# A 48-byte scratch tile declared earlier, so that sixty tiles of SBUF start 64 bytes higher

## What is computed

```python
x = x + tanh(g_xattn[0]) * L0_xattn(layernorm(x), ctx)   # 16 heads of 64, 120 keys per batch
x = x + tanh(g_ffn[0])   * L0_ffn(layernorm(x))          # softmax gate, 8 experts of 256x256, all computed
x = x + tanh(g_xattn[1]) * L1_xattn(layernorm(x), ctx)   # 16 heads of 16, with biases
x = x + tanh(g_ffn[1])   * L1_ffn(layernorm(x))          # 8 routed experts; only the first 512 tokens
```

## The kernel before

| product (step) | stationary, mod 128 | moving, mod 128 | moving columns | matmuls |
|---|---|---|---|---|
| experts (`y_ffn`) | `yT_hi`, `yT_lo`: 0 | `ew_hi`, `ew_lo`: 0 | 512 | 3072 |
| values (`n_v`) | `ctxT_hi`: 96, `ctxT_lo`: 32 | `wv_hi`, `wv_lo`: 0 | 512 | 768 |
| queries (`n_q`) | `wq_hi`, `wq_lo`: 0 | `xT_hi`, `xT_lo`: 32 | 256 | 3072 |
| first output (`x_out`) | `q_hi`, `q_lo`: 32 | `wo_hi`, `wo_lo`: 0 | 256 | 3072 |
| second queries (`y_q`) | `w1_hi` part: 64, `w1_lo` part: 0 | `yT_hi`, `yT_lo`: 0 | 256 | 768 |
| gate (`p_gate`) | `w1_hi`: 0 and 32, `w1_lo`: 64 and 96 | `yT_hi`, `yT_lo`: 0 | 256 | 384 |
| second output (`z_out`) | `q1_hi`, `q1_lo`: 0 | `w1_hi` part: 64, `w1_lo` part: 0 | 256 | 768 |

## Time and profile before

### The profile page before, as it was taken

One profiled execution on the slowest core, in us unless ns is written; L12 is line 12 of the kernel. 1 busy time (PEld: TensorE's weight loads), 2 busy tenths in 40 slices (PEclk: granted clock), 3 DMA queues, 4 the chain that ended last, 5 costly groups with the idle time before them and its releaser, 6 DMA issues.

```text
span 3661.3 us, 96559 instructions
## 1 busy us (share of the span) xinstructions
PE 3607.3 (99%) x34964; PEld 3017.5 (82%) x34964; DVE 2420.4 (66%) x5502; ACT 1718.4 (47%) x3116; POOL 1533.1 (42%) x1718
## 2 busy tenths in 40 slices
PE   7999999999999999999999999999999999999999
PEld 6888888888888888888888888888888888888875
DVE  4666666666666666666666666666666666666676
ACT  4445445445445445445445445445445445445431
POOL 3334334334334334334334334334334334334334
PEclk8999999999999999999999999999999999999999
DMA  2000000000000000000000000000000000000002
GB/s 95 15 15 16 13 14 15 13 14 15 13 14 15 13 14 15 13 14 15 13 14 15 13 14 13 15 13 13 16 13 13 17 13 13 17 13 13 17 26 67
DMA packets 67626, 64.91 MB, mean 18 GB/s; under 512 B 5728, under 2 KB 64896, under 8 KB 67328
## 3 DMA queue, kind: packets, MB, share of 16 engines
q1 hardware_dynamic: 66482, 63.31, 5.4%
q10 hardware_dynamic: 1102, 1.02, 0.1%
HBM read 39.14 MB, written 17.30 MB: 15 GB/s over the span
## 4 chain that ended last, share of the span: by engine, by line
PE 96%; ACT 2%; DVE 1%; issue 0%; DMA 0%; SPq 0%; POOL 0%; POOLq 0%; DVEq 0%; ACTq 0%
PE g L888 38%; PE scores L888 13%; PE g L894 12%; PE g L1043 6%; PE scores L993 5%; PE g L959 4%; PE g L1062 3%; PE scores L1053 3%; PE scores L1027 3%; PE g L908 3%; ACT prob L830 2%; PE g L970 2%; PE scores L997 1%; PE scores L1031 1%; PE g L1122 1%
## 5 line engine op out<-in xcount | busy, mean ns | idle before, releaser
L1383 DVE SCALAR_TENSOR_TENSOR x<-g,lg_ident,x 128x256 f32<-128x256 f32 x1024 | 489.1, 483 | 224.9 <-PE g L888 201.4
L830 ACT ACTIVATE prob<-scores 120x1024 f32<-120x1024 f32 x512 | 501.5, 1024 | 115.1 <-PE scores L1031 67.5
L723 ACT CAST q_hi<-g 128x512 fp32r<-128x512 f32 x256 | 150.1, 586 | 577.2 <-PE g L888 570.3
L888 PE MATMUL g<-ew_hi,yT_hi 128*128 128x512 f32 x1024 | 420.0, 410 | 0.0
L661 POOL TENSOR_TENSOR q_lo<-q_full,q_hi 128x512 fp32r<-128x512 f32 x256 | 327.7, 1290 | 214.4 <-ACT q_full L759 214.3
L888 PE MATMUL g<-ew_lo,yT_hi 128*128 128x512 f32 x1024 | 402.4, 393 | 0.0
L888 PE MATMUL g<-ew_hi,yT_lo 128*128 128x512 f32 x1024 | 399.5, 390 | 0.0
L586 POOL TENSOR_TENSOR y_rstd<-y_mv,eps 128x2 f32<-128x2 f32 x128 | 25.1, 196 | 839.5 <-DVE y_mv L1242 839.5
L1322 DVE TENSOR_REDUCE y_nm<-g 128x4 f32<-128x480 f32 x512 | 300.7, 649 | 111.8 <-PE g L970 111.7
L1322 DVE TENSOR_REDUCE ctx_nm<-g 128x4 f32<-128x480 f32 x512 | 311.8, 651 | 71.8 <-PE g L959 71.7
L666 POOL TENSOR_TENSOR q_lo<-an,q_hi 128x512 fp32r<-128x512 f32 x256 | 326.8, 1288 | 47.4 <-ACT q_hi L859 47.3
(11 more groups left out here) (219 smaller groups left out, 9440.3 us busy)
## 6 DMA issues: line engine op xcount, KB each, us to landing
out<-y_x SPq DMA_DIRECT2D x64, 256.0 KB, 2.1
x_in<-in_x SPq DMA_DIRECT2D x62, 256.0 KB, 2.9
ctx_nm<-in_ctx SPq DMA_DIRECT2D x62, 120.0 KB, 2.6
ctx1T<-ctxT SPq DMA_DIRECT2D x62, 120.0 KB, 1.9
q_full<-in_gu SPq DMA_DIRECT2D x16, 256.0 KB, 3.2
vx<-in_ew SPq DMA_DIRECT2D x4, 512.0 KB, 4.0
wk_s<-in_wk SPq DMA_DIRECT2D x2, 512.0 KB, 5.4
prob<-in_wq SPq DMA_DIRECT2D x1, 1024.0 KB, 6.1
```

Of the source, the lines that this page charges most:

```text
L723: a.copy(dst, ring.bank(job)[:, 0:cols]).then_inc(done.sem, 1)
L830: a.activation(prob[:, e].rearrange("p o u s -> p (o u s)"), scores[0:NK, banks, :].rearrange("p o c -> p (o c)"), ACT.Exp, scale=scale).t ...
L888: ins = t_.matmul(out_, lhsT[u], rhs[v], start=first and n == 1, stop=last and n == 3 * len(terms))
L1383: ins = v.scalar_tensor_tensor(out=x1[:, t, :], in0=ring.bank(Y_FFN[j])[:, o * D:(o + 1) * D], scalar=lg[:, t, 2 * n + o:2 * n + o + 1], i ...
```

## The change

`x_st6`, 2 x 6 float32 values or 48 bytes per partition, is declared next to `x_mv` instead of after `ctx1T`.

```diff
-        x_mv, x_rstd = sb("x_mv", [P, T, 2]), sb("x_rstd", [P, 2, T])
+        x_st6, x_mv, x_rstd = sb("x_st6", [P, T, 6]), sb("x_mv", [P, T, 2]), sb("x_rstd", [P, 2, T])
         neg_half, eps = sb("neg_half", [P, TT]), sb("eps", [P, T])
@@
         ctx1T = sb("ctx1T", [P, KD, NK])
-        x_st6 = sb("x_st6", [P, T, 6])
         eb_s = y_x3[:, 0, :]
```

## The result

| | median | range, runs |
|---|---|---|
| before | 3662.91 us | 3660.32 to 3663.07, 5 |
| after | 3682.66 us | 3680.39 to 3683.17, 5 |

The ratio is 1.0052 with a 95% interval of 1.004 to 1.0064. That is 14.7 to 23.4 us more, and outside the range that was forecast (3653 to 3679 us). The profiled execution after took 3680.31 us.

The account below looks back on a forecast made before the run. The prediction took TensorE's string of matmuls (99% busy) to bound the kernel. Its terms, all taken as 0, added to 3663.01 us gave 3663.0 us, with an 8-in-10 range of 3653 to 3679 us.

Parts of the forecast that it names:

- What bounds the kernel: Whole kernel: a string of matmuls, TensorE 99% busy and 96% of the chain; nothing off TensorE close to counting.
- What the change removes and adds: 0 us: All five engines: same number, order, waits and shapes of instructions, no new wait; 0 us.
- 512 columns, "I take 0": Experts and values on TensorE: address effect taken as 0; possible cost 9.2 to 15.4 us, gain bounded at 7.1 us.
- the same product at two weight addresses: 256-column products: w_lo and w_hi stand 64 bytes apart in the block and their durations do not part; 0 taken.
- 256 columns, "I take 0", bound 1.2 ns: 8064 TensorE matmuls: placements differ by 1.2 ns, 1%; at most 9.7 us either way, taken as 0.
- The signs of being wrong: TensorE: a large group of matmuls moving over 1% in spacing, or a new wait above 5 us.
- The other engines and the store: GpSimd, ScalarE, VectorE: taken as 0, ScalarE's waits at 1.1 us; last store from y_x3: 0, bound 0.2 us.
- The rule on transactions: Last store: a source off a 256-byte multiple needs 5 transactions, not 4; at most 6% longer, an estimated 0.13 us.
- The rule on two read ports: TensorE: weight loading takes no read bandwidth from the running matmul, so operands' relative place is worth 0; not in the sum.
- the rivals: Slower: experts' operand leaves its favourable place, 3678.4 us, chance 0.18; faster: operands at the same place disturb each other, 3653.6 us, 0.12.
- The slower rival: Experts: yT leaves its multiple of 128 bytes, 3072 x 5 ns = 15.4 us more, 3678.4 us; chance 0.18.

Follow-up runs that it names:

- experiment 2: Kernel before, with the 64-byte tile y_sums instead of x_st6 declared before x_mv, raising the following tiles by 64 bytes: 3681.94 us, ratio 1.0047.
- experiment 3: The change with its shift taken back: x_mv and x_rstd go where x_st6 was, large tiles keep the addresses of before; 3663.99 us, ratio 1.0001.
- the first map: Separate program with only split-operand matmuls, 512 then 256 columns, operands at varied distances: 512 columns 226.7 ns at 0, 233.4 at 64 bytes.
- experiment 5: Against the kernel before, x_in to half go up by 64 bytes, x1 and the second half's tiles by 256: 3666.4 us, ratio 1.0006.
- experiment 9: Two placements against the kernel before: q to kmx up 192, vx onward 256, 3658.34 us; xT up 160, q onward 256, 3658.29 us.
- experiment 6: Against the kernel before, tiles from x_in on go up by 128, 192 or 256 bytes: 3674.44, 3665.94 and 3661.38 us.
- experiment 1: Kernel before with x_st6 as the very first tile, so weights and all other operands go up by 64 bytes: 3665.63 us, ratio 1.0003.
- The maps: Two matmul-only programs without the network: the first map, and a second with only 256 columns, where one group ran at 117.8 and 113.3 ns.
- four of the placements: Those that move yT by exactly 256 bytes: experiment 5, 256 bytes in experiment 6, both of experiment 9; the experts gain 1.1 to 3.7 us.

## Why the prediction was wrong

- *What bounds the kernel.* Right: the chain, the waits and the busy shares of the other engines are the same after, and all of the loss is in TensorE's spacing.
- *What the change removes and adds: 0 us.* Right. Experiments 2 and 3 show that `x_st6` and its neighbours have no part in it.
- *512 columns, "I take 0".* This is the step that failed. It had bounded the cost at 9.2 to 15.4 us, and measured it is +12.1 us. It put the term at 0 "since the row of the same product at two weight addresses says so". That comparison was one of 256 columns, and the earlier trace rows show only its `w_lo` half, at distance 128. The `w_hi` half, at 64 and 192, has 282 and 279 ns in the trace against 280 and 280. These three distances happen to be alike: the first map has 117.8, 118.6 and 117.7 ns there. None of them says anything of distance 0 with 512 columns, where the map has 226.7 ns against about 233 at most others. The experts stood at that distance, and the values, the other large product of 512 columns, did not. The stretch read for them was also the wrong one: it began right after a break, where they ran at 231 ns. Their steady 226.7 ns, beside the values' 234, would have shown a difference of 7 ns.
- *256 columns, "I take 0", bound 1.2 ns.* This term failed too. The bound for one matmul was too small: the queries lost 9.6 us, about 3 ns each. They came to distance 160, at which no product of 256 columns of the kernel before stood; the earlier trace rows held other distances. In the map's table it is the second worst value (119.7 ns against 116.6 at 224). That all the 256-column products together lost 9.5 us, just under the 9.7 of the bound, is luck: the bound spread 1.2 ns over 8064 matmuls, and the loss is 3 ns on 3072 of them. The first output, from 32 to 96, gained 1.2 us where the map would have had it lose 1.8: the map is no exact forecast for 256 columns, and 1.2 us is within the scatter.
- *The signs of being wrong.* One of them came: the prediction named a large group whose spacing moves by over 1%, and the experts' steady spacing moved by 2.9% (226.7 to 233.3 ns) and the queries' by 2.5% (117.1 to 120.0). The other, a new wait of TensorE above 5 us, did not.
- *The other engines and the store.* GpSimd's pair is at 988 and 991 ns, and ScalarE's at 361 and 366 ns, within 2 ns of the earlier trace rows. The last store, from its issue to the end of the span, takes 2.55 us after (3676.01 to 3678.56) and took 2.48 before. The median of the 64 stores' landing is 2.2 instead of 2.1 us on the page, and 2.165 instead of 2.10 by the trace's nanoseconds:

```profile
L634 POOL TENSOR_TENSOR kbd_lo<-k_lo,own_row 128x480 fp32r<-128x480 f32 x64 | 63.4, 991 | 0.0
...
L634 POOL TENSOR_TENSOR kbd_hi<-k_hi,own_row 128x480 fp32r<-128x480 f32 x64 | 63.2, 988 | 362.4 <-DVE k_lo L1307 362.4
...
L731 ACT CAST ctxT_hi<-g 128x240 fp32r<-128x240 f32 x64 | 23.4, 366 | 0.0
L730 ACT COPY ctxT<-g 128x240 f32<-128x240 f32 x64 | 23.1, 361 | 24.8 <-PE g L917 24.8
```

```profile
out<-y_x SPq DMA_DIRECT2D x64, 256.0 KB, 2.2
...
3676.01 0.37 SPq L522 DMA_DIRECT2D out<-y_x  x1
```

  The experiments isolate this difference of 0.06 us. In the six traces in which `y_x3` starts at a multiple of 256 bytes (before, experiments 3, 5 and 9, and 256 bytes in experiment 6) the median is 2.10 us; in the six with it 64, 128 or 192 bytes past one it is 2.16 to 2.17 us. The two stores from `wk_s` per trace are less clear: 2.10 us in four of these six, but 2.16 in experiment 1, where `wk_s` moves by 64 bytes too, and also in experiment 2, where it does not. So the term that was taken as 0 is 0.06 us, within its bound of 0.2. The rule on transactions in the Trainium skill ("DMA: Bandwidth & Descriptors", "How a descriptor splits into AXI transactions") had the direction right, and the 0.13 us that the prediction estimated from it are twice the measured value, which moreover does not grow from 64 to 192 bytes.
- *The rule on two read ports* (the Trainium skill, "TensorE: Matmul & The Clock Gate", "Step-by-step: what each phase is for") was used to lower the rivals' chances. The maps go against it as a rule on time: with nothing but weight loads and matmuls on the engines, the spacing depends on the distance between what is loaded and what is streamed (226.7 ns at 0, 233.4 at 64 bytes). Whether read bandwidth is the reason no run shows.
- *The slower rival* was right in direction, in place and nearly in size (15.4 us for the experts against 12.1). Its reason was not: not the place of `yT` in a block of 128 bytes counts (experiment 1 leaves it at 64 and loses nothing), but its distance from `ew`, modulo 256 bytes. Its price lacked the queries' 9.6 us; part of them was made up by -3.6 us in the transposes and -1.7 in the values, so that its 3678.4 us came near the measured time partly by luck.

What stays open is why the distance acts so, what picks between the two spacings of 256 columns, and what sets how soon a stretch of experts settles on its steady spacing, which was worth 1 to 4 us in four of the placements.

## What to carry to other kernels

Where TensorE is the bound and both operands are split float32 as here, addresses are part of the kernel: before a tile is added, moved or resized ahead of large operands, note the distance of stationary from moving operand modulo 256 bytes for each large product, and keep it. Read the spacing of the starts in the steady part of a run, not durations or the first few after a break. A comparison between placements speaks only for the shape and the distances that it holds; where the placement to be forecast is not among them, measure it alone.

## What the runs showed of the hardware

- The steady spacing of split float32 matmuls of 512 columns at full granted clock (1.0 in both maps) depends on the distance between stationary and moving operand with a period of 256 bytes: in one map the 16 values of 0 to 240 bytes recur at 256 to 496 bytes within 0.1 ns.
- With 512 columns: 226.7 ns at 0 and 226.6 at 240 bytes, 228.7 at 192, 230.0 at 176, and 231.9 to 234.1 ns at the twelve others.
- With 256 columns one and the same group can run at 113.3 or at 117.8 ns a matmul; it is not shown what selects.
- Moving both operands together by 64 to 448 bytes changed the 512-column spacing by less than 0.1 ns.
- A store of 256 KB took 2.10 us to land with its source at a multiple of 256 bytes and 2.16 to 2.17 us at 64, 128 or 192 bytes past one (medians of 64 stores, six traces each).
